# Chunk layout of the key halves, the order of the grams, and the place of the query projection in a one-core layer kernel

## The reference, cut to what matters

```python
x_norm = rmsnorm(x)                       # the kernel is given x after a layer norm
k = elu(x_norm @ Wk.T) + 1                # 64 features a token
v = x_norm @ Wv.T                         # 128 a token
def step(M, (k_t, v_t)):                  # M is 64 x 128, 2048 steps
    surprise = norm(v_t - k_t @ M)
    M = M + eta * surprise * outer(k_t, v_t)
    return (M - mean(M)) / sqrt(var(M) + 1e-5)
q = elu(x_norm @ Wq.T) + 1
out = x + (q @ M_last) @ Wout.T
```

## Time and profile before

| | us |
|---|---|
| median of 3 runs | 294.96 |
| the three runs | 292.35, 294.96, 294.99 |
| the profiled execution | 292.8 |
| its span, first to last instruction | 290.9 |
| PE busy | 264.4 (91%) |
| DVE busy | 219.3 (75%) |
| ACT busy | 191.2 (66%) |
| POOL busy | 99.9 (34%) |
| mean granted TensorE clock, of full speed | 0.988 |

### The profile page before, as it was taken

One profiled execution on the slowest core, in us unless ns is written; L12 is line 12 of the kernel. 1 busy time (PEld: TensorE's weight loads), 2 busy tenths in 40 slices (PEclk: granted clock), 3 DMA queues, 4 the chain that ended last, 5 costly groups with the idle time before them and its releaser, 6 DMA issues.

```text
span 290.9 us, 5378 instructions
## 1 busy us (share of the span) xinstructions
PE 264.4 (91%) x1787; PEld 168.0 (58%) x1790; DVE 219.3 (75%) x738; ACT 191.2 (66%) x458; POOL 99.9 (34%) x122
## 2 busy tenths in 40 slices
PE   6899978797699957978999999999999999999993
PEld 2377963243265633565778787776797444444483
DVE  6957579999777568958899987887765566666674
ACT  1539874656345456777876679999782877777740
POOL 9200200000000005898886349998885000000000
PEclk9999997999799999999999999999999999999999
DMA  7600000000000037040000000000000000000005
GB/s 203 189 10 2 2 2 1 0 1 0 0 3 0 1 133 303 2 144 0 5 1 0 2 2 1 0 2 1 0 2 0 2 0 1 0 2 1 0 2 146
DMA packets 8287, 8.51 MB, mean 29 GB/s; under 512 B 1729, under 2 KB 7362, under 8 KB 7746
## 3 DMA queue, kind: packets, MB, share of 16 engines
q1 hardware_dynamic: 7826, 7.84, 8.4%
q10 hardware_dynamic: 432, 0.30, 0.4%
HBM read 7.09 MB, written 1.05 MB: 28 GB/s over the span
## 4 chain that ended last, share of the span: by engine, by line
PE 66%; DVE 22%; ACT 5%; issue 4%; DMA 1%; DVEq 0%; SPq 0%; ACTq 0%
PE PS L796 10%; PE PS L797 10%; PE PS L754 8%; PE PS L734 7%; PE PS L745 3%; PE PS L459 3%; PE PS L582 3%; PE PS L474 2%; DVE arena L1654 2%; DVE arena L1653 2%; DVE mxb L1669 2%; PE PS L577 2%; DMA x<-L_attn_x 1%; PE PS L578 1%; PE PS L579 1%
## 5 line engine op out<-in xcount | busy, mean ns | idle before, releaser
L796 PE MATMUL PS<-arena 128*128 128x512 f16 x128 | 48.5, 379 | 0.6 <-issue 0.6
L797 PE MATMUL PS<-arena 128*128 128x512 f16 x128 | 48.5, 379 | 0.0
L1722 DVE TENSOR_TENSOR arena<-arena 128x512 f32<-128x512 f32 x32 | 22.2, 693 | 19.5 <-ACT arena L1156 19.5
L734 PE MATMUL PS<-arena 128*128 128x512 f32 (+3 forms) x80 | 32.1, 532 | 0.1
L1155 ACT ACTIVATE arena<-PS,arena 128x512 f32<-128x512 f32 x32 | 22.0, 688 | 13.2 <-PE PS L797 13.2
L1198 POOL TENSOR_TENSOR arena<-arena 128x256 f32<-128x256 f32 x32 | 21.5, 673 | 16.8 <-DVE arena L1661 14.4
L1129 ACT ACTIVATE arena<-PS,lnt 128x512 f32<-128x512 f32 (+3 forms) x40 | 24.9, 633 | 2.6 <-DVE lnt L1676 2.5
L1206 POOL CAST arena<-arena 128x512 f16<-128x512 f32 x2 | 1.2, 609 | 73.8 <-ACT x L1020 73.8
L1199 POOL TENSOR_TENSOR arena<-arena,small 128x256 f16<-128x256 f32 (+1 forms) x36 | 23.8, 660 | 2.8
L1669 DVE TENSOR_REDUCE mxb<-PS 128x1 f32<-128x512 f32 (+3 forms) x40 | 22.1, 601 | 0.2 <-PE PS L736 0.2
L1156 ACT ACTIVATE arena<-PS,arena 128x512 f16<-128x512 f32 x32 | 21.8, 681 | 0.0
(11 more groups left out here) (279 smaller groups left out, 635.5 us busy)
## 6 DMA issues: line engine op xcount, KB each, us to landing
arena<-h_T SPq DMA_DIRECT2D x2, 1024.0 KB, 6.0
x<-L_attn_x SPq DMA_DIRECT2D x4, 256.0 KB, 4.6
arena<-cos SPq DMA_DIRECT2D x1, 1024.0 KB, 5.6
arena<-sin SPq DMA_DIRECT2D x1, 1024.0 KB, 7.7
out<-arena SPq DMA_DIRECT2D x4, 256.0 KB, 2.3
arena<-w_T SPq DMA_DIRECT2D x3, 256.0 KB, 3.3
con<-shape_constants ACTq DMA_DIRECT2D x1, 192.0 KB, 3.4
w1e<-L_ffn_W SPq DMA_DIRECT2D x1, 128.0 KB
```

Of the source, the lines that this page charges most:

```text
L734: i = mm(PS[:, k, 0:cnt * P], qT1[:, t * P:(t + 1) * P], kT1[:, c * P:(c + cnt) * P], start=True, stop=not last)
L796: mm(bank(u % 8), wH[:, k, m * P:(m + 1) * P], sH[:, k, cols], start=(k == 0), stop=False)
L797: i = mm(bank(u % 8), wL[:, k, m * P:(m + 1) * P], sL[:, k, cols], start=False, stop=(k == HT4 - 1))
L1722: v.tensor_tensor(RP[m], FP[m], high, ALU.subtract).then_inc(rest_ready, 1)
```

## The change

The two halves of the keys' partitions now hold alternate chunks: partitions 0 to 63 chunks 0 and 2, partitions 64 to 127 chunks 1 and 3. There are 64 blocks, none in both halves. `keys(g)` projects chunks 2g and 2g+1 into the two row halves of one bank. Blocks whose neighbour lies in the other half (31 and 63) get it by `next_keys`, six small copies on ScalarE. The keys' grams have runs of 15, 15, 15, 15 and 4 blocks; the first two need chunks 0 and 1 alone and stand ahead of the values' grams runs 2 to 4. Chunk 2 of the turned tokens is scaled by ScalarE instead of VectorE. The queries are projected behind the lane transposes, into banks 4 and 5; `QE` has its own place; their sum is made by VectorE in eight parts, in steps 16 to 23 of the loop, instead of by GpSimd; the hidden layer's matmuls also wait for `qphi_act`. Two of the hidden layer's eight results are read ahead of the loop, six in steps 0 to 5. The fallback path's copies of the keys follow the new layout. In the diff, of replaced function bodies only the new lines stand.

```diff
-SH = S // 2 + 1
+SH = S // 2
-EH_LATE = 3
+EH_LATE = 6
+SB_AT = 3
+Q_AT = 16
-        QT, QE = take(T // 2), xT[:, 0:T // 2]
+        QT, QE = take(T // 2), take(T // 2)
...
-        V_RUNS = [(b, s0, min(26, S - s0)) for b, s0 in zip((7, 0, 1, 2, 3), range(0, S, 26))]
-        KU_RUNS = [(b, c0, min(15, SH - c0)) for b, c0 in zip((7, 4, 5, 6, 2), range(0, SH, 15))]
+        V_RUNS = [(b, s0, min(26, S - s0)) for b, s0 in zip((7, 6, 0, 1, 2), range(0, S, 26))]
+        KU_RUNS = [(3, (*range(0, 15),)), (7, (*range(15, 30),)), (4, (*range(32, 47),)), (6, (*range(47, 62),)), (5, (30, 31, 62, 63))]
+        def gram_lanes(r, h):
+            b, blocks = KU_RUNS[r]
+            have = PS[0:2 * L, b, 0:len(blocks) * 2 * (HALF + 1)]
+            if len(blocks) == 4:
+                return (G[0:2 * L, :, :].rearrange("p j (g h i) -> p g h i j", g=2, h=2)[:, :, h, K2 - 2:K2, :],
+                        have.rearrange("p (g i h j) -> p g i h j", g=2, i=2, h=2)[:, :, :, h, :])
+            s0 = blocks[0] // K2 * 2 * K2 + K2 * h + blocks[0] % K2
+            return (G[0:2 * L, :, s0:s0 + len(blocks)].rearrange("p j s -> p s j"),
+                    have.rearrange("p (c h j) -> p c h j", c=len(blocks), h=2)[:, :, h, :])
...
             def values(ch):
+                (pe.wait_ge(xrt_act, ch + 1) if ch < 3 else pe.wait_ge(xrt_dve, 1))
                 mm(bank(ch), wvT[:, :], xrT[:, ch * BANK:(ch + 1) * BANK], start=True, stop=True).then_inc(v_done, 1)
+            def keys(g):
+                for h in range(2):
+                    ch = 2 * g + h
+                    i = mm(PS[F * h:F * h + F, 4 + g, :], wkT[:, :], xrT[:, ch * BANK:(ch + 1) * BANK], start=True, stop=True)
+                i.then_inc(k_done, 1)
             def values_gram(r):
@@ -461,48 +474,42 @@
             def keys_gram(r):
+                b, blocks = KU_RUNS[r]
                 pe.wait_ge(ku_ready, 3 if r < 2 else 6)
+                pe.wait_ge(ku_act, (2, 2, 4, 4, 10)[r])
                 if r == 0:
+                    pe.wait_ge(vt_dve, 2)
+                if r == 1:
                     pe.wait_ge(vgram_act, 1)
+                if r == 2:
+                    pe.wait_ge(k_ready, 1)
+                if r == 3:
+                    pe.wait_ge(vgram_act, 2)
+                if r == 4:
                     pe.wait_ge(k_ready, 2)
+                for k, c in enumerate(blocks):
+                    i = mm(PS[0:2 * L, b, k * 2 * (HALF + 1):(k + 1) * 2 * (HALF + 1)], KU[:, c, :, :].rearrange("p t i -> p (t i)"),
                            UX[:, c, :, :].rearrange("p h j -> p (h j)"), start=True, stop=True)
                 i.then_inc(gram_done, 1)
             turned_in(0)
             values(0)
             values(1)
+            keys(0)
             pe.wait_ge(set_once, SET)
             values_gram(0)
             turned_in(1)
             values_gram(1)
             values(2)
             values(3)
+            keys(1)
+            keys_gram(0)
+            keys_gram(1)
             for r in range(2, 5):
                 values_gram(r)
+            for r in range(2, 5):
                 keys_gram(r)
             pe.wait_ge(vgram_act, 5)
             pe.wait_ge(gram_act, 3)
             pe.wait_ge(gram_dve, 2)
...
                     i = tr(PS[0:W, b, (r - r0) * 3 * L:(r - r0 + 1) * 3 * L], G[0:3 * L, (r - 1) % (HALF + 1), 0:W], ident[0:3 * L, 0:3 * L])
                 i.then_inc(lanes_done, 1)
+            pe.wait_ge(late_in, 32)
+            for b in range(2):
+                for hf in range(2):
+                    ch = 2 * b + hf
+                    i = mm(PS[64 * hf:64 * hf + F, 4 + b, :], wqT[:, :], xrT[:, ch * BANK:(ch + 1) * BANK], start=True, stop=True)
+            i.then_inc(q_done, 1)
             pe.wait_ge(xn_ready, NT)
             for n in range(NT):
                 if n % 4 == 0:
@@ -529,6 +543,7 @@
             pe.wait_ge(moe_in, 64)
             pe.wait_ge(xnt_act, 4)
             pe.wait_ge(last_act, 4)
+            pe.wait_ge(qphi_act, 2)
             for h in range(2):
                 for ch in range(4):
                     mm(bank((4, 0)[h] + ch), w1e[:, h * P:(h + 1) * P], xT[:, ch * BANK:(ch + 1) * BANK], start=True, stop=True).then_inc(eh_done, 1)
...
             f(small[:, 39:40], normw[:, 0:1], ACT.Exp)
+            def keys(g):
+                act.wait_ge(k_done, g + 1)
+                e = KE[:, g * BANK:(g + 1) * BANK]
+                o.need(o.did(f(e, bank(4 + g), ACT.Relu, scale=-1.0)))
+                f(e, e, ACT.Exp, scale=-1.0).then_inc(kphi_act, 1)
+            def scaled_keys(g):
+                c0, c1 = K2 * g, K2 * (g + 1)
+                act.wait_ge(k_ready, g + 1)
+                if g == 0:
+                    act.wait_ge(eta_set, 1)
+                f(KU[:, c0:c1, 1, 0:HALF], KU[:, c0:c1, 0, 0:HALF], ACT.Copy, scale=etac[:, 0:1]).then_inc(ku_act, 1)
+                f(KU[:, c0:c1 - 1, 1, HALF:L], KU[:, c0 + 1:c1, 0, 0:HALF], ACT.Copy, scale=etac[:, 0:1]).then_inc(ku_act, 1)
+            def next_keys(h, g):
+                c = K2 * (g + h)
+                h0, h1 = slice(F * h, F * h + F), slice(F * (1 - h), F * (1 - h) + F)
+                f(KU[h0, K2 * (g + 1) - 1, 0, HALF:L], KU[h1, c, 0, 0:HALF], ACT.Copy).then_inc(ku_act, 1)
+                f(KU[h0, K2 * (g + 1) - 1, 1, HALF:L], KU[h1, c, 0, 0:HALF], ACT.Copy, scale=etac[h1, 0:1]).then_inc(ku_act, 1)
+            def keys_gram(r):
+                act.wait_ge(gram_done, r + 1)
+                for h in range(2):
+                    i = f(*gram_lanes(r, h), ACT.Copy)
+                i.then_inc(gram_act, 1)
+            keys(0)
+            act.wait_ge(xrt_done, 3)
+            f(xrT[:, 2 * BANK:3 * BANK], bank(2), ACT.Copy, scale=normw[:, 0:1]).then_inc(xrt_act, 1)
             act.wait_ge(xrt_done, 4)
             values_gram(0)
+            scaled_keys(0)
             values_gram(1)
+            keys(1)
+            keys_gram(0)
+            scaled_keys(1)
+            for h, g in ((0, 0), (0, 1), (1, 0)):
+                next_keys(h, g)
+            for r in range(2, 5):
+                values_gram(r)
+            keys_gram(2)
+            keys_gram(4)
+            for b, (r0, cnt) in enumerate(LANE_RUNS):
+                act.wait_ge(lanes_done, b + 1)
+                f(CC[:, 0:3, r0:r0 + cnt, :], PS[0:W, b, 0:cnt * 3 * L].rearrange("p (j q t) -> p q j t", q=3, t=L), ACT.Copy).then_inc(lanes_act, 1)
+            zq = PS[:, 4:6, :].rearrange("p b c -> p (b c)")
             act.wait_ge(q_done, 1)
             f(QT, zq, ACT.Relu).then_inc(qphi_act, 1)
             n = o.did(f(QE, zq, ACT.Relu, scale=-1.0))
             o.need(n)
             f(QE, QE, ACT.Exp, scale=-1.0).then_inc(qphi_act, 1)
             def surprise(j):
...
-            act.wait_ge(q_ready, 1)
-                    hidden(1, 4 - EH_LATE + j)
-                if j == EH_LATE:
+                    hidden((8 - EH_LATE + j) // 4, (8 - EH_LATE + j) % 4)
+                if j == SB_AT:
...
-            pool.wait_ge(qphi_act, 2)
-            tt(QT, QT, QE, ALU.add).then_inc(q_ready, 1)
...
                 dve.wait_ge(v_done, ch + 1)
                 v.tensor_copy(VT[:, ch * BANK:(ch + 1) * BANK], bank(ch)).then_inc(vt_dve, 1)
+            def keys(g):
+                c0, c1 = K2 * g, K2 * (g + 1)
+                z = bank(4 + g).rearrange("p (c i) -> p c i", i=HALF)
+                dve.wait_ge(kphi_act, g + 1)
                 v.scalar_tensor_tensor(out=KU[:, c0:c1, 0, 0:HALF], in0=z, scalar=0.0, in1=KE[:, c0 * HALF:c1 * HALF].rearrange("p (c i) -> p c i", i=HALF),
                                        op0=ALU.max, op1=ALU.add).then_inc(k_ready, 1)
+                if g == 0:
+                    dve.wait_ge(early_in, 16 * 4)
+                    dve.wait_ge(xrt_done, 4)
+                    v.tensor_scalar(xrT[:, 3 * BANK:T], bank(3), normw[:, 0:1], None, ALU.mult).then_inc(xrt_dve, 1)
+                dve.wait_ge(k_ready, g + 1)
+                v.tensor_copy(KU[:, c0:c1 - 1, 0, HALF:L], KU[:, c0 + 1:c1, 0, 0:HALF]).then_inc(ku_ready, 1)
+                for h in range(2):
+                    h0 = slice(F * h, F * h + F)
+                    v.tensor_scalar(UX[h0, c0:c1, h, 0:HALF], KU[h0, c0:c1, 0, 0:HALF], etac[h0, 0:1], None, ALU.mult).then_inc(ku_ready, 1)
+            keys(0)
             values(2)
             values(3)
             keys(1)
             for n in range(NT):
...
+                    if j == Q_AT:
+                        dve.wait_ge(qphi_act, 2)
+                    part = slice((j - Q_AT) * P, (j - Q_AT + 1) * P)
+                    v.tensor_tensor(QT[:, part], QT[:, part], QE[:, part], ALU.add).then_inc(q_ready, 1)
```

More of the change, by code:

```diff
@@ L480, in _ @@
             values(1)
-            keys(0, 0)
-            keys(0, 1)
+            keys(0)
             pe.wait_ge(set_once, SET)
@@ L488, in _ @@
             values(3)
[L489 to L492, removed]
+            keys(1)
+            keys_gram(0)
+            keys_gram(1)
             for r in range(2, 5):
```

(39 more changed lines are left out.)

38 lines of the change are left out of this document (2 added, 36 removed).

## The result

The changed kernel takes 290.15 us (median of 6 runs, 289.33 to 290.61) against 294.16 us (median of 6 runs, 292.35 to 297.44). The ratio is 0.9855, 95% interval 0.9813 to 0.9898: faster by 1.0 to 1.9%. The profiled executions stand at 290.06 and 292.8, only 2.7 us apart, so part of the 4.0 between the medians is in runs of the kernel before that its profile does not show; experiment 7 bears on that part.

The account below looks back on a forecast made before the run. TensorE bounds the stretch ahead of the lanes without a gap. Lanes 3.65 us earlier less a 0.5 stall gives 3.15 us; from 293.8, the middle of the known times, that is 290.6, range 287.9 to 293.0.

Parts of the forecast that it names:

- Ahead of the lanes: TensorE's stretch before the lane transposes: key pairs save 1.93 us, moved queries 1.87; lanes start 3.65 us earlier.
- The stall of 0.27: Keys' gram run 0 waits for VectorE to empty bank 3, starting at 21.25 instead of 20.98.
- Behind the lanes: Lane transposes, queries, ScalarE's work and table load precede the hidden layer, which starts at 44.76, 0.26 later than before.
- the stall for TensorE's first sum: Step 3 on VectorE waits for TensorE's bank 4 sum, done at 54.50: 0.67 us at most, 0.5 taken.
- about nothing: First loop step: ScalarE's read of the second hidden result, 47.69 to 48.3, delays the square root wanted at 48.44 by nothing.
- The clock rule of the Trainium skill: TensorE idling 4.4 us before the hidden layer makes low clock certain; the stall then 0.7 to 1.1 instead of 0.5.
- Rival B: Lanes' gain comes, but low clock, queries' parts and ScalarE give back 1.5 to 2 us; gain 1.3 to 2; chance 0.22.
- C: TensorE stays at the lower clock through the whole hidden layer: 4.0 us slower, 296.8; chance 0.04.
- D: Key pairs do not run side by side, or run 0's waits are 2 us late: 1.2 gained, 292.5; chance 0.04.
- E: Low clock stretch falls into idle time and a later one disappears: 4 to 5 us gained, 288.5; chance 0.04.
- The queries' parts: VectorE's eight parts of the queries' sum in loop steps, 0.20 us each, hide in idle time; at 0.34 they cost 0.6.
- The drain that the Trainium skill speaks of: Changing tiling mode drains TensorE; queries between transposes add two changes, so something behind the lanes; no size given.

Follow-up runs that it names:

- experiment 7: Kernel before plus 9 warming (dummy) matmuls ahead of the hidden layer and 12 in step 13: median 292.76 us, ratio 0.9934 to the kernel before.
- experiment 1: Changed kernel with the query projection and its relu and exp back ahead of the keys' grams 2 to 4: median 292.72 us, ratio 0.9881 to the kernel before.
- experiment 9: Kernel of experiment 1 plus 9 warming matmuls ahead of the hidden layer and 12 in step 13: 290.78 us, ratio 0.9852 to the kernel before.
- experiment 2: Changed kernel with values and keys of a chunk alternating, so key pairs never run side by side: median 293.42 us, ratio 0.9908 to the kernel before.
- experiment 8: Changed kernel with the keys' gram runs 0 and 1 behind the values' runs 2 to 4 instead of ahead: median 291.61 us.
- experiment 4: Changed kernel with one hidden result instead of two read ahead of the loop (EH_LATE 7): median 290.53 us, ratio 0.9831 to the kernel before.
- experiment 3: Changed kernel plus 18 warming matmuls in TensorE's idle time ahead of the hidden layer: median 291.03 us, ratio 0.9862 to the kernel before.
- experiment 5: Changed kernel plus 18 warming matmuls ahead of the hidden layer and 12 in step 13: median 289.10 us, ratio 0.9804 to the kernel before.
- experiment 6: The changed kernel timed again, unaltered, in the experiments' rounds: 290.48 us, ratio 0.9870 to the kernel before.

## Why the prediction was right

**Ahead of the lanes.** Forecast 3.65 us, measured 3.61. The pairs took 1.01 each, not 0.93, which cost 0.16. The stall of 0.27 that I had put ahead of run 0 was not there: VectorE copied chunk 3 from 20.27 to 20.96, and by TensorE's timeline run 0 started at 21.10, right behind the second pair. The two errors nearly cancel. The chains show the parts: queries 1.87, and keys 1.86 + 1.94 against two times 1.01, thus 1.78. Experiments 1 and 9 confirm the first (1.73 and 1.79 us at the lanes). Experiment 2 confirms that the pairing is the second: 2.37, or about 1.7 without its eight times 0.08. By experiment 8 the order of the grams is no gain. The 1.94 include the two matmuls of 16 tokens that the new layout does without; no run prices them by themselves. Nor does one isolate the six `next_keys` copies or ScalarE's scaling of chunk 2, but the chain has neither on it.

**Behind the lanes.** The hidden layer starts at 45.18, forecast 44.76: ScalarE began the queries 0.19 us later, its three instructions took 3.05 instead of 2.93 up to the table load, and from there on it was 4.14 instead of 4.03.

**The term that was mis-sized** is the stall for TensorE's first sum, 0.5 in the sum, 1.41 measured. My bound of 0.67 had that sum done at 54.50; it was done at 55.30. Of the 0.80 between them half is the hidden layer's later start (0.42) and half its length, 9.08 us instead of 8.67. The prediction also missed where the loss would show. Of the first step it said "about nothing", and that step lost 1.00 of the 1.41, because the second result came 3.79 us behind the start of the hidden layer and not 2.93: the clock was low from its first matmul on, not from its second. By experiment 4 that 1.00 is not to be added to the stall; without it step 3 waits longer. The clock rule of the Trainium skill ("TensorE: Matmul & The Clock Gate", "Why this matters for your kernels") spoke against the change, and the trace agrees: half the clock behind 4.59 us of idling, and 1.42 us back when experiment 3 fills the gap. The 1.1 that I had put as the most under that rule was still too small. Rival B had this mechanism, and the loop alone lost nearly what B said (1.5 to 2); the time at the end did not.

**Behind the loop** the changed kernel gained where I expected nothing. From the last scan's 2.16 to 2.74 us of the profiled times there are 0.58. Of these, 0.18 are TensorE's shorter lateness at the loop's end (0.25 us instead of 0.43). The attention stage, from the first score to the first matmul of the next layer, lasted 97.2 us in the kernel before and 96.4 in the changed one, but the stage ahead of it took 0.4 more. In later profiles the attention stage was 96.4 to 96.9 for either kernel, so this looks like a difference between executions and not like a gain of the change. I did not find its cause.

**The number.** The forecast of 290.6 is 0.45 from the measured 290.15, and in part by luck. At the last scan the gain is 2.16 us where the sum has 3.15, short mostly by the 0.9 of the mis-sized stall; 0.58 behind the loop made 2.74 of it in the profiled times (290.06, forecast 289.65). The medians are 4.0 apart, more than the sum. Which of the pairs of the kernel before would be met I had left open. Experiment 7 shows that warming takes 1.9 us (0.8 to 3.1) off that kernel with nothing moved on the loop's path. It is not simply that the changed kernel has less low clock: its runs with a mean of 0.976 to 0.982 took 289.3 to 290.6 us, those of the kernel before with 0.976 to 0.982 took 293.4 to 295.8. Where the low stretches fall counts. Why the changed kernel, with the same idle time there, meets the long low stretch more rarely than the kernels of experiments 1 and 8 is open; I tried nothing that moves that stretch alone.

**Rivals.** C did not come: the low stretch ended during the hidden layer. D is out by the pairs' 1.01 us. E (288.5) did not come either; only with warming are single runs that fast. The queries' parts hid, as forecast: the eight steps with a part are none over 0.01 us longer than before. The drain that the Trainium skill speaks of ("TensorEngine Tiling (Array Packing)", "Key Properties") is seen at most as the 0.08 us of experiment 2; weight loads could be its cause as well, so that is not shown to be a drain.

## What to carry to other kernels

Two f32 matmuls of 64-column weights into opposite row halves of a bank took 1.01 us here where two into the same half took 1.86, if they stood side by side, so lay out data so that they can. Work moved off the critical stretch lands in front of something; look what has lost its distance there, and whether TensorE's clock will have fallen while it waits for it. When two waits in a row both lose time, ask whether the later one has a fixed time of its own: then curing the first brings nothing (experiment 4). A few dummy matmuls in TensorE's idle gaps were worth 1.4 us on the path (experiment 3) and 1.4 us in the changed kernel's median (experiments 5 and 6), and they narrowed the runs of the kernel before from 4.9 to 1.4 us.

## What the runs showed of the hardware that I had not expected

- A low granted clock did not end when matmuls ran: 10.2 us at 0.53 with TensorE busy for 8.8 of them (experiment 1). Executions of the kernel before differed by up to 4.9 us in time, from 0.988 to 0.961 in mean granted clock.
- 18 matmuls in bf16 ahead of the hidden layer kept the clock at the upper level (1.00 from 41 to 52 us, experiment 5), and so did 9 (1.00 from 41 to 53, experiment 7); 12 did so in step 13 (1.00 from 69.8 to 80, experiment 5). In both profiles the clock was low later, behind the loop.
- Alternating a 128-column and a 64-column f32 matmul, each with its own weights, cost about 0.08 us each, 1.02 in the mean against 0.94.
- An f32 sum of 128x128 on VectorE showed 0.28 us of its own, and the next scan started 0.36 behind its start.
